# Node stage of a two-layer graph network: the second normalisation moved from VectorE to ScalarE

## Chip, cores and metric

The kernel runs on one core of a Trainium2 chip. The metric is the device time of one execution in microseconds (us), as the median of several runs.

## What is computed

There are 12500 nodes with 128 features and 200000 edges sorted by destination. Two layers follow each other. The first sums weighted neighbour rows per source node, sends the sums and the node's own row through a linear map with bias and relu, normalises both, adds them to the input row and normalises the row again. The second gathers a linear image of those rows per edge, and so on. The part that matters here is the end of the first layer:

```
h    = relu(feat_neigh @ W_neigh.T + b_neigh)                 # per node, 128 features
base = x + first branch + offsets
y    = base + scale * (h - mean(h)) / sqrt(var(h) + 1e-9)     # first normalisation (of h)
x1   = (y - mean(y)) / sqrt(var(y) + 1e-5)                    # second normalisation (of y)
f    = x1 @ node_w * attr                                     # rows for the second layer
```

## The kernel before

The program has four parts in order of time: a short set-up, a first edge stage (until about 3072 us), the **node stage** (3072 to 3357 us), a second edge stage (3357 to 5345 us) and a final stage over the nodes (to the end). The parts are separated by barriers, so a microsecond that the node stage takes more or less goes straight to the end.

The node stage cuts the 12500 rows into 25 blocks of 512 rows: 128 partitions with CB = 4 rows of 128 features each. Every engine runs its own list of instructions in order, written as a function `body(b)` that is called for b = 0, 1, 2, ... by `sweep` (unrolled before body 8 and after body 23, a loop between). A body handles several blocks of different age, and semaphores order the engines. `done(engine, signal, m)` waits until block m has given the signal. For block m the work is:

- SyncE loads the first of four tables of sums into `t_in` (L768), GpSimd adds the other three with accumulating DMAs in its bodies m+1, m+3 and m+5 (L789).
- TensorE, body m: 4 transposes of `t_in` (L811). Body m+1: bias and linear map into `ps_mm` (L818, L821), after the transposes of block m+1. Body m+4: 4 transposes of x1 out of `pack` (L829). Body m+5: 8 multiplications with `node_w` (L836).
- ScalarE, body b, in this order: clear a piece of `table` (L853), copy `nT` of block b (L856), relu of block b-1 into `h` (L861), square root for the h of block b-2, square root for the y of block b-3 (both L846, function `root`), copy `x1T` of block b-4 (L868), two DMA issues for block b-6 (L872, L873), eight scaled copies of block b-5 into `pack` and `f_sb` (L879, L881).
- VectorE, body b, in this order: `statistics` of the h of block b-2 and of the y of block b-3 (L892, L897, L901), then `centre` for the h of block b-2, then `centre` for the y of block b-3. A `centre` waits for the square root, takes the reciprocal (L905), refines it by one Newton step of three small instructions (L93, L95, L97; `refine`), and writes (row - mean) * rs with 4 instructions (L909), for h in place and for y into `pack`.
- GpSimd, body m+8: once h of block m is centred, y = h * scale (L796), y = y + base (L800); then, in its next body, three more accumulating DMAs.

The wait of ScalarE for `m_x1` does not exist before the change: x1 is VectorE's, and TensorE (L829) and GpSimd wait for it. The final stage already has a normalisation of the other form: VectorE makes a bias `nb` = -mean * rs (L1258), and ScalarE writes 4 copies with that bias and scale (L1214).

Of the kernel before, what the change touches and what calls it, by code (L numbers as in the profile page):

```python
# [15 lines left out]
ALU = mybir.AluOpType  # L16
ACT = mybir.ActivationFunctionType
# [20 lines left out]
NP = P  # L38
CB = 4
# [29 lines left out]
def at(s, q, j, back, ring=UN):  # L69

    return s - back, q + (j - back) // ring, (j - back) % ring
# [7 lines left out]
def done(eng, signal, step, back=0):  # L79

    if not isinstance(step, int) or step >= back:
        eng.wait_ge(signal, step - back + 1)  # L82


def uses(eng, signal, rnd, each):

    if not isinstance(rnd, int) or rnd > 0:
        eng.wait_ge(signal, rnd * each)


def refine(dve, v, r0, t, r, steps, m):

    dve.scalar_tensor_tensor(out=t[:, 0, :], in0=r0, scalar=-0.5, in1=v, op0=ALU.mult, op1=ALU.mult).then_inc(steps, 1)  # L93
    dve.wait_ge(steps, m * 3 + 1)
    dve.tensor_tensor(t[:, 1, :], t[:, 0, :], r0, ALU.mult).then_inc(steps, 1)  # L95
    dve.wait_ge(steps, m * 3 + 2)
    dve.scalar_tensor_tensor(out=r, in0=t[:, 1, :], scalar=1.5, in1=r0, op0=ALU.add, op1=ALU.mult).then_inc(steps, 1)  # L97
    dve.wait_ge(steps, m * 3 + 3)


def graph_layers(nc, a, out):
    with ExitStack() as ctx:
# [3 lines left out]
        def sem(name):  # L106
            return ctx.enter_context(nc.semaphore(name))

        def bank(name, shape, scope):
            return scope.enter_context(nc.psum_tensor(name, shape, F32))  # L110
# [40 lines left out]
        with ExitStack() as s0:  # L151
            def tmp(name, shape, dt=F32):
                return s0.enter_context(nc.sbuf_tensor(name, shape, dt))
# [8 lines left out]
            rows = tmp("rows", [1, 4, D])  # L162
# [202 lines left out]
        def live(b):  # L365
            return not isinstance(b, int) or 0 <= b < NB
# [23 lines left out]
        with ExitStack() as s2:  # L390
# [31 lines left out]
            mv = tmp("mv_s", [NP, HC, 2])  # L422
# [4 lines left out]
            rs = tmp("rs_s", [NP, HC])  # L427
# [293 lines left out]
        with ExitStack() as s3:  # L721
# [7 lines left out]
            y = tmp("y_m", [NP, 2, CB, D])  # L729
            pack = tmp("pack", [NP, UN, CB, 2, D])  # L730
# [3 lines left out]
            mv = tmp("mv_m", [NP, 2, CB, 2])  # L734
# [2 lines left out]
            r0 = tmp("r0_m", [NP, 2, CB])  # L737
            nw = tmp("nw_m", [NP, 2, 2, CB])
            rs = tmp("rs_m", [NP, 2, CB])
            ps_m = [bank(f"ps_mm{i}", [NP, CB, D], s3) for i in range(2)]  # L740
            ps_n = bank("ps_mn", [P, CB, P], s3)
            ps_t = bank("ps_mt", [P, CB, P], s3)
# [2 lines left out]
            pk_st = [sem(f"m_pk_st{i}") for i in range(UN)]  # L745
# [9 lines left out]
            m_cen, m_hs, m_y, m_x1 = sem("m_cen"), sem("m_hs"), sem("m_y"), sem("m_x1")  # L755
# [6 lines left out]
            with nc.Block() as block:  # L762
# [77 lines left out]
                @block.scalar  # L840
                def _(act):
                    def root(m, which):
                        if live(m):
                            done(act, m_var[which], m)
                            done(act, m_rs[which], m, 1)
                            act.activation(sd[:, which, :], var[:, which, :], ACT.Sqrt).then_inc(m_sd[which], 1)  # L846

                    clear = table[:, :, :].rearrange("p g n -> p (g n)")
                    act.wait_ge(m_blank, 1)

                    def body(b, q, j):
                        if live(b):
                            act.copy(clear[:, bass.ds(b * (2 * NT // NB), 2 * NT // NB)], blank[:, :]).then_inc(cleared, 1)  # L853
                            done(act, m_sum, b)
                            done(act, m_mm, b, 2)
                            act.copy(nT[:, j % 2, :, :], ps_n[:, :, 0:NP]).then_inc(m_nT, 1)  # L856
                        m, r, i = at(b, q, j, 1)
                        if live(m):
                            done(act, m_mm, m)
                            done(act, m_hs, m, 2)  # L860
                            act.activation(h[:, i % 2, :, :], ps_m[i % 2][:, :, :], ACT.Relu).then_inc(m_relu, 1)  # L861
                        root(b - 2, 0)
                        root(b - 3, 1)
                        m, r, i = at(b, q, j, 4)
                        if live(m):
                            done(act, m_tr, m)
                            done(act, m_f, m, 2)
                            act.copy(x1T[:, i % 2, :, :], ps_t[:, :, 0:NP]).then_inc(m_x1T, 1)  # L868
                        m, r, i = at(b, q, j, 6)
                        if live(m):  # L870
                            done(act, m_pk, m)
                            act.dma_start(rows_of(xs_d, m), pack[:, i, :, :, :].rearrange("p c g d -> p (c g d)")).then_inc(pk_st[i], 16)  # L872
                            act.dma_start(rows_of(f_d, m), flat(f_sb[:, i, :, :])).then_inc(pk_st[i], 16)  # L873
                        m, r, i = at(b, q, j, 5)
                        if live(m):
                            done(act, m_f, m)
                            uses(act, pk_st[i], r, 32)
                            for c in range(CB):
                                act.activation(pack[:, i, c, 1, :], ps_f[i % 2][:, c, 0:D], ACT.Copy,  # L879
                                               scale=attr_s[:, bass.ds(m * CB + c, 1)])  # L880
                                last = act.activation(f_sb[:, i, c, :], ps_f[i % 2][:, c, D:2 * D], ACT.Copy,  # L881
                                                      scale=attr_s[:, bass.ds(m * CB + c, 1)])
                            last.then_inc(m_pk, 1)
                    sweep(act, body, 0, NB + 6, 8, 24)
                    for i in range(UN):
                        act.wait_ge(pk_st[i], 32 * len(range(i, NB, UN)))

                @block.vector
                def _(dve):
                    def statistics(m, rows, which, eps):  # L890
                        for c in range(CB):
                            last = dve.bn_stats(st6[:, which, c, :], rows[:, c, :])  # L892
                        last.then_inc(m_st[which], 1)
                        dve.wait_ge(m_st[which], m * 2 + 1)
                        settle(dve, passed)
                        for c in range(CB):
                            last = dve.bn_aggr(mv[:, which, c, :], st6[:, which, c, :])  # L897
                        last.then_inc(m_st[which], 1)
                        dve.wait_ge(m_st[which], m * 2 + 2)
                        done(dve, m_sd[which], m, 1)  # L900
                        dve.tensor_scalar(var[:, which, :], mv[:, which, :, 1], eps, None, ALU.add).then_inc(m_var[which], 1)  # L901

                    def centre(m, rows, to, which):
                        done(dve, m_sd[which], m)
                        dve.reciprocal(r0[:, which, :], sd[:, which, :]).then_inc(m_rs[which], 1)  # L905
                        done(dve, m_rs[which], m)
                        refine(dve, var[:, which, :], r0[:, which, :], nw[:, which, :, :], rs[:, which, :], m_nw[which], m)
                        for c in range(CB):
                            last = dve.tensor_scalar(to[:, c, :], rows[:, c, :], mv[:, which, c, 0:1], rs[:, which, c:c + 1],  # L909
                                                     ALU.subtract, ALU.mult)  # L910
                        return last

                    def body(b, q, j):
                        m1, r1, i1 = at(b, q, j, 2)
                        m2, r2, i2 = at(b, q, j, 3)
                        if live(m1):
                            done(dve, m_relu, m1)
                            statistics(m1, h[:, i1 % 2, :, :], 0, 1e-9)
                        if live(m2):
                            done(dve, m_y, m2)  # L920
                            statistics(m2, y[:, i2 % 2, :, :], 1, 1e-5)
                        if live(m1):
                            k = i1 % 2
                            centre(m1, h[:, k, :, :], h[:, k, :, :], 0).then_inc(m_cen, 1)
                        if live(m2):
                            uses(dve, pk_st[i2], r2, 32)
                            centre(m2, y[:, i2 % 2, :, :], pack[:, i2, :, 0, :], 1).then_inc(m_x1, 1)
                    sweep(dve, body, 0, NB + 3, 8, 24)


# [361 lines left out]
```

## Time and profile before

| | us |
|---|---|
| median of 3 runs (5498.08 to 5500.08) | 5498.28 |
| the profiled execution | 5497.89 |
| its span in the trace | 5496.1 |
| node stage in it, 3072 to 3357 | 285 |

The span is that of the trace; the profiled execution's own time is 1.8 us longer. In the rows below, a row of the timeline gives the start, the duration (for several merged instructions from the first start to the last end), the engine, the line, what is written and read, the count, and in brackets the idle time of the engine before it and what ended it. PE is TensorE, PEld its weight loads, DVE VectorE, ACT ScalarE, ACTq the queue of ScalarE where it issues DMAs, POOL GpSimd. Successive instructions of an engine overlap by a part of their duration, so what one costs its engine in a row of equals is the distance between starts.

### The profile page before, as it was taken

To read this page: it belongs to the slowest core of one execution; us is meant where nothing else is said; L and a number is where in the kernel's file an instruction comes from. 1 tells how busy PE (TensorE), PEld (TensorE's weight loads), DVE (VectorE), ACT (ScalarE), POOL (GpSimd) and SP (SyncE) were. 2 spreads that over 40 slices of the span, in tenths; PEclk is the share of its full clock that TensorE was granted. 3 is DMA by queue.
4 is the path that set the end of the run, shared out by engine and by line. 5 is a ranking of instruction groups with operands and counts; after the bars stand their busy time and mean duration, and the time that the engine had idled before them with its cause. 6 is when DMAs were issued, how large, how long until landed. Compare 5 with 4: busy or idle time off the path is not lost. (4 is left out here: it accounts for less than half of the span.)

```text
span 5496.1 us, 83091 instructions
## 1 busy us (share of the span) xinstructions
PE 3528.2 (64%) x18413; PEld 2923.1 (53%) x18413; DVE 2741.1 (50%) x11175; ACT 2615.7 (48%) x9201; POOL 4067.5 (74%) x3277
## 2 busy tenths in 40 slices
PE   1555555555555555555555377888888888888872
PEld 0443343344334334334434255888888888888871
DVE  2655555555565555565555384333333333333338
ACT  0322222222222222222222255888888888888863
POOL 0888888888888888888888654777777777777750
PEclk9766666666666666676677577777777777777765
DMA  8666666666666666666665683333333333333323
GB/s 225 120 117 111 111 116 114 112 112 112 111 117 115 111 111 115 116 111 112 112 113 99 130 204 105 81 81 79 81 81 79 81 81 81 79 81 81 79 74 127
DMA packets 748229, 588.07 MB, mean 107 GB/s; under 512 B 336911, under 2 KB 616360, under 8 KB 745111
## 3 DMA queue, kind: packets, MB, share of 16 engines
q0 software_dynamic: 286576, 224.93, 29.6%
q1 hardware_dynamic: 446066, 310.47, 20.9%
q10 hardware_dynamic: 15542, 52.19, 2.4%
q8 instruction: 13, 0.21, 0.0%
q14 instruction: 32, 0.26, 0.0%
HBM read 374.65 MB, written 212.60 MB: 107 GB/s over the span
## 5 line engine op out<-in xcount | busy, mean ns | idle before, releaser
L705 POOL DMA_INDIRECT sums_scratch<-vals,to_i x1568 | 2447.4, 1561 | 616.5 <-issue 506.4
L992 POOL DMA_INDIRECT fg<-f_scratch,src_e x1568 | 1486.4, 948 | 501.6 <-issue 477.3
L1045 ACT ACTIVATE hot<-raw,e_s 128x40 f32<-128x40 f32 x6272 | 1392.3, 313 | 346.2 <-DVE raw L1068 317.5
L619 PE MATMUL ps_n<-same,hot 128*40 128x128 f32 x3136 | 694.3, 414 | 1326.8 <-issue 1324.9
L619 PEld LDWEIGHTS ps_n<-same,hot 128*40 128x40 f32 x3136 | 556.0, 184 | 1436.2 <-issue 1371.8
L662 ACT COPY near<-ps_n 40x512 f32<-40x512 f32 x196 | 113.3, 578 | 1636.3 <-PE ps_n L619 1636.3
L1021 PE MATMUL ps_eu<-hot,prod 128*128 128x120 f32 x3136 | 889.3, 378 | 0.0
L1019 PEld LDWEIGHTS ps_eu<-hot,prod 128*128 128x128 f32 x3136 | 622.3, 244 | 305.4 <-DVE prod L1075 253.9
L1074 DVE TENSOR_TENSOR prod<-ps_ew,fg 128x256 f32<-128x256 f32 x392 | 164.6, 420 | 1239.3 <-DMA fg<-f_scratch,src_e 1239.3
L1019 PE MATMUL ps_eu<-hot,prod 128*128 128x40 f32 x3136 | 618.9, 288 | 248.0 <-DVE prod L1075 247.0
L1021 PEld LDWEIGHTS ps_eu<-hot,prod 128*128 128x128 f32 x3136 | 619.6, 245 | 0.0
L586 DVE TENSOR_TENSOR to_i<-away,srcf 128x8 int32<-128x8 f32 x196 | 33.0, 169 | 1119.4 <-POOLq L76 1119.3
L573 DVE SCALAR_TENSOR_TENSOR junk<-srow_s,srcf,lower 128x128 f32<-128x128 int32 x1568 | 582.1, 437 | 0.0
L1008 PE MATMUL ps_ew<-fc_w,hid_e 128*128 128x256 f32 x1568 | 495.1, 472 | 13.3 <-DMA hid_e<-hid_scratch 13.3
L632 PEld LDWEIGHTS ps_v<-xw_s,near 40*128 40x128 f32 x3136 | 368.7, 190 | 205.4 <-issue 127.4
L632 PE MATMUL ps_v<-xw_s,near 40*128 40x128 f32 x3136 | 406.2, 280 | 0.9 <-ACT vals L673 0.9
L1008 PEld LDWEIGHTS ps_ew<-fc_w,hid_e 128*128 128x128 f32 x1568 | 365.3, 245 | 71.4 <-DMA hid_e<-hid_scratch 13.7
L561 DVE TENSOR_SCALAR same<-srow_s,srcf 128x128 f32<-128x128 int32 x1568 | 399.6, 340 | 4.5
L1075 DVE TENSOR_TENSOR prod<-ps_ew,fg 128x768 f32<-128x768 f32 x392 | 371.6, 948 | 0.0
L566 DVE TENSOR_SCALAR hot<-iota_f,rel,ew_s 128x40 f32<-128x40 f32 x1568 | 353.0, 340 | 0.0
L624 PE MATMUL ps_eh<-eT,fc_w 128*128 128x512 f32 x392 | 306.5, 873 | 0.0
L1030 PE MATMUL ps_ec<-sums,lin_w 128*128 128x80 f32 x1568 | 273.3, 335 | 0.0
(193 smaller groups left out, 3833.8 us busy)
## 6 DMA issues: line engine op xcount, KB each, us to landing
srow_s<-in_src SPq DMA_DIRECT2D x196, 512.0 KB, 3.5
e_s<-in_edge_attr SPq DMA_DIRECT2D x196, 256.0 KB, 3.7
hid_scratch<-hid SPq DMA_DIRECT2D x196, 256.0 KB, 3.6
hid_e<-hid_scratch SPq DMA_DIRECT2D x196, 256.0 KB
sums_scratch<-zeros ACTq DMA_DIRECT2D x24, 1056.0 KB, 26.8
sums_scratch<-vals,to_i POOLq DMA_INDIRECT x1568
fg<-f_scratch,src_e POOLq DMA_INDIRECT x1568
t_in<-sums_scratch POOLq DMA_DIRECT2D x72, 256.0 KB, 6.7
```

The costliest lines, as they stand in the source:

```text
L561: last = dve.tensor_scalar(same[:, k, t, :], rows[:, t // TH, t % TH, :], srcf[:, t:t + 1], None, ALU.is_equal)
L566: last = dve.tensor_scalar(hot[:, k, t, :], iota_f[:, 0:W], rel[:, t // TH, t % TH:t % TH + 1], ew_s[:, j, t:t + 1], ALU.is_equal, ALU.mult)
L573: last = dve.scalar_tensor_tensor(out=junk[:, t, :], in0=rows[:, t // TH, t % TH, :], scalar=srcf[:, t:t + 1], in1=lower[:, :], op0=ALU.is ...
L619: last = pe.matmul(ps_n[t // TH][:, t % TH, :], hot[:, k, t, :], same[:, k, t, :], start=True, stop=True)
L632: last = pe.matmul(ps_v[t // TH][:, t % TH, :], near[:, k, t, :], xw_s[:, i, t // TH, :], start=True, stop=True)
L705: pool.indirect_dma_start(out=sums_d[i], out_offset=bass.IndirectOffsetOnAxis(ap=to_i[:, j, t:t + 1], axis=0), in_=vals[:, j, t, :], in_of ...
L992: pool.indirect_dma_start(out=fg[:, j, t, :], out_offset=None, in_=f_d, in_offset=bass.IndirectOffsetOnAxis(ap=src_s[:, j, t:t + 1], axis= ...
L1008: last = pe.matmul(ps_w[k][:, 2 * t:2 * t + 2, :, :], hid[:, j, t, :], fc2_w[:, :], start=True, stop=True)
L1019: pe.matmul(ps_u[k][:, hf, 0, :], prod[:, k, t, 0, :], hot[:, k, t, 0, :], start=(t == 0), stop=False, skip_group_check=True)
L1021: last = pe.matmul(ps_u[k][:, hf, 1:4, :], prod[:, k, t, 1, :], hot[:, k, t, 1:4, :], start=False, stop=(t == TS - 1), skip_group_check=True)
L1045: last = act.activation(hot[:, k, t, c, :], raw[:, k, t, :], ACT.Copy, scale=e4_s[:, j, t, c:c + 1])
L1075: last = dve.tensor_tensor(prod[:, k, :, g, MUL:D].rearrange("p t (d u) -> p t d u", d=3), ps_w[k][:, :, 2 + g, None, :].to_broadcast([P, ...
```

## The change

VectorE no longer writes x1. It does the reciprocal and the refinement for y, then makes nb = -mean * rs, a 128x4 instruction, and signals `m_nb`. ScalarE waits for `m_nb` of block b-3 in its body b, behind the two square roots and ahead of the x1T copy, and writes the four 128x128 pieces of x1 as Identity with bias nb and scale rs. The wait for the store of the `pack` slot moves along with the writes. VectorE waits, ahead of the reciprocal for y, that ScalarE has written x1 of the block before, since `rs` and `nb` have one buffer. The additional `k = i1 % 2` changes nothing.

```diff
+            nb = tmp("nb_m", [NP, CB])
+            m_nb = sem("m_nb")
...
                         root(b - 2, 0)
                         root(b - 3, 1)
+                        m, r, i = at(b, q, j, 3)
+                        if live(m):
+                            done(act, m_nb, m)
+                            uses(act, pk_st[i], r, 32)
+                            for c in range(CB):
+                                last = act.activation(pack[:, i, c, 0, :], y[:, i % 2, c, :], ACT.Identity,
+                                                      bias=nb[:, c:c + 1], scale=rs[:, 1, c:c + 1])
+                            last.then_inc(m_x1, 1)
                         m, r, i = at(b, q, j, 4)
                         if live(m):
                             done(act, m_tr, m)
...
-                    def centre(m, rows, to, which):
+                    def inverse(m, which):
                         done(dve, m_sd[which], m)
                         dve.reciprocal(r0[:, which, :], sd[:, which, :]).then_inc(m_rs[which], 1)
                         done(dve, m_rs[which], m)
                         refine(dve, var[:, which, :], r0[:, which, :], nw[:, which, :, :], rs[:, which, :], m_nw[which], m)
+
+                    def centre(m, rows, to, which):
+                        inverse(m, which)
                         for c in range(CB):
...
                         if live(m2):
-                            uses(dve, pk_st[i2], r2, 32)
-                            centre(m2, y[:, i2 % 2, :, :], pack[:, i2, :, 0, :], 1).then_inc(m_x1, 1)
+                            done(dve, m_x1, m2, 1)
+                            inverse(m2, 1)
+                            dve.scalar_tensor_tensor(out=nb[:, :], in0=mv[:, 1, :, 0], scalar=-1.0, in1=rs[:, 1, :],
+                                                     op0=ALU.mult, op1=ALU.mult).then_inc(m_nb, 1)
```

## Rows read from the trace of the kernel before

**Rows 1.** Busy time by stretch: the node stage, and its late part.

```profile
core 0: us, PE busy (x) PEld busy (x) DVE busy (x) ACT busy (x) POOL busy (x), PEclk, DMA share, GB/s
3072.00:3357.00 285.00, 184.10 (x650) 128.17 (x650) 200.72 (x850) 125.50 (x350) 129.31 (x126) 0.69 0.73 182
3265.00:3317.00 52.00, 41.76 (x161) 30.05 (x160) 47.92 (x199) 29.94 (x86) 23.06 (x21) 0.76 0.55 150
```

**Rows 2.** Groups by line in the node stage: the transposes of the sums.

```profile
L811 PE MATMUL ps_mn<-ident,t_in 128*128 128x128 f32 x100 | 22.0, 360 | 128.0 <-DMA t_in<-sums_scratch 128.0
```

**Rows 3.** Timeline, VectorE, from one body's first reciprocal (body 14) to the next.

```profile
3223.90 0.18 DVE L905 RECIPROCAL r_m<-sd_m 128x4 f32<-128x4 f32 x1 [1.46 <-ACT sd_m L846]
...
3225.94 1.25 DVE L93 SCALAR_TENSOR_TENSOR nw_m<-r_m,var_m 128x4 f32<-128x4 f32 x1
...
3227.41 1.12 DVE L97 SCALAR_TENSOR_TENSOR rs_m<-nw_m,r_m 128x4 f32<-128x4 f32 x1
3228.57 1.11 DVE L909 TENSOR_SCALAR pack<-y_m,mv_m,rs_m 128x128 f32<-128x128 f32 x4
3229.60 0.86 DVE L892 BATCH_NORM_STATS2 st_m<-h_m 128x6 f32<-128x128 f32 x4
...
3232.62 0.17 DVE L905 RECIPROCAL r_m<-sd_m 128x4 f32<-128x4 f32 x1
```

**Rows 4.** Timeline, ScalarE: a pair from body 13, then bodies 14 and 15.

```profile
3213.86 0.57 ACT L868 COPY x1T<-ps_mt 128x512 f32<-128x512 f32 x1
...
3215.15 0.37 ACT L879 ACTIVATE pack<-ps_mf,attr_s 128x128 f32<-128x128 f32 x1 [0.72 <-issue]
...
3223.67 0.29 ACT L846 ACTIVATE sd_m<-var_m 128x4 f32<-128x4 f32 x2
3224.03 0.58 ACT L868 COPY x1T<-ps_mt 128x512 f32<-128x512 f32 x1
...
3227.54 0.37 ACT L879 ACTIVATE pack<-ps_mf,attr_s 128x128 f32<-128x128 f32 x1 [2.93 <-PE ps_mf L836]
...
3229.55 1.10 ACT L853 COPY table<-blank 128x1024 f32 x1
3230.49 0.65 ACT L856 COPY nT<-ps_mn 128x512 f32<-128x512 f32 x1
3230.97 0.67 ACT L861 ACTIVATE h_m<-ps_mm 128x512 f32<-128x512 f32 x1
3231.45 0.27 ACT L846 ACTIVATE sd_m<-var_m 128x4 f32<-128x4 f32 x1
```

**Rows 5.** Timeline, GpSimd and TensorE: from a centred h to the next sums.

```profile
3206.90 1.26 POOL L796 TENSOR_TENSOR y_m<-h_m,vecs 128x512 f32<-128x512 f32 x1 [5.28 <-DVE h_m L909]
...
3209.46 2.63 POOL L789 DMA_DIRECT2D t_in<-sums_scratch  x3
...
3218.02 1.11 PE L811 MATMUL ps_mn<-ident,t_in 128*128 128x128 f32 x4 [4.89 <-DMA t_in<-sums_scratch]
```

**Rows 6.** Timeline of the final stage: its bias on VectorE, its copies on ScalarE.

```profile
5409.60 0.16 DVE L1258 SCALAR_TENSOR_TENSOR nb_f<-mv_f,rs_f 128x4 f32<-128x4 f32 x1
...
5409.88 0.88 ACT L1214 ACTIVATE o_sb<-y_f,nb_f,rs_f 128x128 f32<-128x128 f32 x2 [3.20 <-DVE nb_f L1258]
5410.59 0.34 ACTq L1224 DMA_DIRECT2D out<-o_sb  x1
5410.66 0.86 ACT L1214 ACTIVATE o_sb<-y_f,nb_f,rs_f 128x128 f32<-128x128 f32 x2
5411.44 0.19 ACT L1220 ACTIVATE sd_f<-var_f 128x4 f32<-128x4 f32 x1
```

**Rows 7.** Timeline: first reciprocals of bodies 4 and 27, and the stage's last DMA issue.

```profile
3128.98 0.18 DVE L905 RECIPROCAL r_m<-sd_m 128x4 f32<-128x4 f32 x1 [4.45 <-ACT sd_m L846]
...
3342.61 0.18 DVE L905 RECIPROCAL r_m<-sd_m 128x4 f32<-128x4 f32 x1 [0.34 <-ACT sd_m L846]
...
3354.20 0.46 ACTq L873 DMA_DIRECT2D f_scratch<-f_sb  x1
```

More of the change, by code:

```diff
@@ L915, in body @@
                         m2, r2, i2 = at(b, q, j, 3)
+                        k = i1 % 2
                         if live(m1):
```

## The prediction

> **What bounds the kernel now.** I read the busy time by stretch first: the edit lies in the node stage alone, 285 us of the 5496.1 us span, in which VectorE is busy 201 us, ScalarE 125 us, and no engine is full [rows 1]. A stage in which nothing is full is bound by a ring of waits, so I went on to the timeline of one body on each engine, which I follow by the moment at which VectorE starts the body's first reciprocal (for h). In the middle of the stage it comes after 8.7 us and after 10.3 us by turns, 19.0 us for two bodies. Two things set it:
>
> - VectorE's own list. From the reciprocal at 3223.90 to the one at 3232.62 it never stops: 8.72 us [rows 3]. Two instructions of 128x4 take 1.25 and 1.12 us in it, as long as GpSimd's two multiplications and additions of y run beside them, where the same line takes 0.16 us elsewhere. The y half, from the first reciprocal to the first write of x1, is over 4.67 us after the body's start (3223.90 to 3228.57); the four writes themselves cost 1.03 us (3228.57 to 3229.60).
> - A ring through the sums. h is centred, GpSimd makes y (3206.90), issues the DMAs of the block four later (3209.46), TensorE gets them at 3218.02 [rows 5], then the linear map, relu and the square root of the block before lead to the reciprocal at 3223.90 [rows 3]. That is 17.0 us, and the 2.0 us from a reciprocal to GpSimd's start (3223.90 to 3225.94, where L93 begins to be held) make it 19.0 us for two bodies. The transposes waited 128 us for these DMAs in the stage, its start included [rows 2].
>
> ScalarE is on neither for long: in body 14 its copies started after 2.93 us of idling [rows 4].
>
> **The change, part by part.**
>
> 1. VectorE loses the four writes, 1.03 us a body [rows 3], and gains nb, 0.16 us with some 0.04 us of gap, as in the final stage [rows 6]. Its list shrinks from 8.72 to about 7.9 us. The nb instruction stands behind L97, which GpSimd's second operation has just released, so I give it 0.16 us; were it held as L93 is, it would be 1.25 us, which I keep for the range.
> 2. VectorE's new wait for x1 of the block before costs nothing: ScalarE wrote that in its body before, ahead of the square root that this body has already waited for.
> 3. ScalarE gains four Identity instructions. The final stage shows the same shape and operands: starts at 5409.88 and 5410.66 for two pairs, and the next instruction at 5411.44, so 1.56 us for four [rows 6]. The lower bound is the pitch of its copies with a scale alone, eight in 2.01 us (3227.54 to 3229.55), 1.0 us for four [rows 4]. I take 1.55, since function, source and operands are the same.
> 4. ScalarE gains a wait, and this decides. The wait for nb of block b-3 is met only at the **end** of VectorE's body b. Behind it in ScalarE's list stand all that the next body needs: x1T, two DMA issues, eight copies, the clear, nT, relu, and then the square root for which VectorE's body b+1 waits ahead of its first reciprocal. So the two lists, which ran side by side, now run one after the other: VectorE from the square root to nb, ScalarE from nb to the next square root.
>
> The sum for one turn of this new ring:
>
> - reciprocal to nb's start: 4.67 [rows 3]
> - nb's start to the first Identity: 0.28 (5409.60 to 5409.88) [rows 6]
> - four Identity: 1.55
> - x1T to the first copy: 0.48 to 1.29. Before it was 1.29 (3213.86 to 3215.15) with 0.72 idle for issue, since the queue put two DMA issues between [rows 4]. In the final stage a DMA issue goes out at 5410.59 while two Identity and a square root ahead of it are still to start [rows 6], so the queue runs ahead of its engine; here it has the 1.55 us of the Identities for that. I take 0.48, what a 128x512 copy costs in a row (3230.49 to 3230.97), and keep 1.29 for the range.
> - eight copies: 2.01; clear to nT: 0.94; nT to relu: 0.48; relu to square root: 0.48 (3229.55, 3230.49, 3230.97, 3231.45) [rows 4]
> - square root to reciprocal: 0.23 (3223.67 to 3223.90) [rows 4, 3]
>
> Together 11.1 us a body. VectorE's statistics of the next body (3.0 us, 3229.60 to 3232.62) lie beside ScalarE's 6.2 us and cost nothing. The ring through the sums needs 19.0 us for two bodies against 22.2 now, so it and TensorE's work fall into slack of 3 us.
>
> **The whole stage.** Body 4 starts, as before, at 3128.98 [rows 7], since it waits for the first DMAs of the ring. In body 4 ScalarE has no copies yet: 4.67 + 0.28 + 1.55 + 0.48 + 0.94 + 0.48 + 0.48 + 0.23 = 9.1, so body 5 starts at 3138.1, and with copies body 6 at 3149.2. Eighteen full turns of 11.1 lead to body 24 at 3349.0. Body 25 has no clear and no nT (9.7), bodies 26 and 27 no relu either (9.2 each): body 27 at 3377.1, against 3342.61 before [rows 7]. From there to the last DMA issue it was 11.6 us (3354.20); the wait chain at the end is nearly the same, with the four Identity in place of the four writes: plus 0.5. So the stage ends about **35 us** later, and the barrier behind it passes that on whole. Against the profiled execution's 5497.89 us that gives 5532.9; the median of the runs is 0.39 higher, and I put 5533.
>
> A page of the Trainium skill speaks the other way. Perfetto Trace Analysis, Optimizing Scalar/DVE Operations, says that where VectorE is saturated, offloading some of its work to ScalarE may make sense. By it this change should pay; the price that it would have here is the second rival's.
>
> **The rivals.**
>
> - *The ring with unhidden issues.* As forecast, but ScalarE's queue doesn't run ahead through the Identities: 0.8 us more in each of 21 turns, plus 17 us: 5550. For it: the 0.72 us of issue [rows 4]. Against it: the DMA issue between the Identities [rows 6]. Chance 0.13.
> - *The offload pays.* VectorE is at 47.9 of 52 us in the late part of the stage, ScalarE at 29.9 [rows 1]. There VectorE's list is the only bound, over the nine bodies from 3265 us on; if ScalarE took x1 without delaying the square root, each of these would be 0.83 us shorter, about 7 us in all, and at most 0.83 in each of 24, 20 us: 5491, at best 5478. The ring through the sums has no x1 in it and would not shorten. It decides from the point where the x1 copies end early enough that the next square root is ready when VectorE has its statistics, 3.0 us after nb; the list above needs 6.2 after the first Identity starts. For it only the low share of ScalarE, which is an average. Chance 0.03.
> - *No difference.* ScalarE's new wait falls into its idle time (2.93 us ahead of the copies in every second body [rows 4]) and the old ring stays the bound: 5498. Against it: that slack is used up by the Identities and the wait (nb at about 3228.7, when the copies had already begun at 3227.54), and the other body has none. Chance 0.04.
>
> The forecast has the remaining 0.80.
>
> **Range and chances.** The low end takes Identity at the copies' pitch (0.55 less in 21 turns, 11.5 us: plus 23) and some overlap that I don't see, 5512. The high end takes unhidden issues (5550) and a part of a held nb, 5556. This leaves out little more than the two rivals without a ring. A measurement of this kernel can tell about 0.2%, 11 us, from no change. The ring in either form is slower by more than that: 0.93. Within 0.2%: 0.04. Faster by over 0.2%: 0.03.
>
> **What the profile after would show.** If right: in the timeline of a middle body the first Identity starts 0.3 us behind nb, and ScalarE then runs without a gap to the square root; VectorE is idle some 3 us ahead of every first reciprocal, released by the square root, and the turn is 11.1 us in every body without the alternation; TensorE's wait for the DMAs shrinks and its wait for ScalarE grows. The stage takes about 320 us. If the DMA issues are not hidden there is idle time for issue between x1T and the first copy, and 11.9 us a turn. I am wrong if a first reciprocal follows the statistics without a gap, if the stage is no longer than 296 us, or if stages other than the node stage change by more than a microsecond or two.

## The result and the profile after

| | before | changed |
|---|---|---|
| median, us | 5498.28 (5 runs, 5496.1 to 5500.08) | 5527.75 (5 runs, 5526.98 to 5530.41) |
| span of the profiled execution, us | 5496.1 | 5525.2 |

The changed kernel is slower by 29.5 us: the ratio is 1.0057, with a 95% interval from 1.0044 to 1.0069. That is more than the 0.2% that a measurement of this kernel can tell.

First the busy time by stretch of the changed kernel; the first row is its node stage, the second its middle, the third its second edge stage (columns: length of the stretch, then busy time and count of instructions of each engine, clock, DMA share, GB/s):

```profile
core 0: us, PE busy (x) PEld busy (x) DVE busy (x) ACT busy (x) POOL busy (x), PEclk, DMA share, GB/s
3072.00:3392.00 320.00, 199.89 (x650) 137.66 (x650) 179.16 (x775) 158.24 (x450) 129.28 (x126) 0.64 0.64 160
3128.00:3265.00 137.00, 100.74 (x324) 69.57 (x323) 90.25 (x383) 74.08 (x211) 62.87 (x62) 0.66 0.72 175
3387.00:5375.00 1988.00, 1730.24 (x9800) 1614.80 (x9800) 684.49 (x1572) 1626.12 (x7262) 1479.79 (x1568) 0.76 0.32 81
```

VectorE lost 22 us of busy time (costed for 25 blocks: 21) and ScalarE gained 33 (costed: 39) [rows 1]. No engine is full: ScalarE is busy for 158 of 320 us, VectorE for 179. But ScalarE's gain is close to what the stage grew by, so busy time alone can't tell the added work from a wait. TensorE's granted clock was 0.64 in the stage where it was 0.69, and its busy time grew by 16 us, to 200. The waits say where the time is. This is the list of who waited for whom in the changed kernel's node stage (total us, times, longest):

```profile
POOL y_m L798 <- DVE h_m L922: 159.8, 25, 12.6
PE ps_mn L813 <- DMA t_in<-sums_scratch: 127.4, 21, 70.3
ACT pack L871 <- DVE nb_m L942: 116.6, 25, 4.9
PEld ps_mn L813 <- DMA t_in<-sums_scratch: 90.9, 7, 70.6
DVE r_m L915 <- ACT sd_m L848: 75.8, 25, 5.4
```

And the last of these in the kernel before:

```profile
DVE r_m L905 <- ACT sd_m L846: 21.4, 10, 5.2
```

ScalarE waits 25 times for nb, 4.7 us each time on average, and VectorE 25 times for ScalarE's square root, 3 us each, where it waited 10 times before. Waits of each engine for the other in every body are what two lists give that run one after the other; the timeline shows whether they do. One turn of that on VectorE, from the timeline, with a first reciprocal at either end:

```profile
3217.11 0.18 DVE L915 RECIPROCAL r_m<-sd_m 128x4 f32<-128x4 f32 x1 [2.83 <-ACT sd_m L848]
...
3219.15 1.24 DVE L93 SCALAR_TENSOR_TENSOR nw_m<-r_m,var_m 128x4 f32<-128x4 f32 x1
...
3220.62 1.12 DVE L97 SCALAR_TENSOR_TENSOR rs_m<-nw_m,r_m 128x4 f32<-128x4 f32 x1
...
3221.77 0.16 DVE L942 SCALAR_TENSOR_TENSOR nb_m<-mv_m,rs_m 128x4 f32<-128x4 f32 x1
3221.85 0.86 DVE L902 BATCH_NORM_STATS2 st_m<-h_m 128x6 f32<-128x128 f32 x4
...
3228.28 0.18 DVE L915 RECIPROCAL r_m<-sd_m 128x4 f32<-128x4 f32 x1 [3.31 <-ACT sd_m L848]
```

And the same turn on ScalarE:

```profile
3222.05 0.49 ACT L871 ACTIVATE pack<-y_m,nb_m,rs_m 128x128 f32<-128x128 f32 x1 [4.88 <-DVE nb_m L942]
3222.41 0.34 ACTq L882 DMA_DIRECT2D xs_scratch<-pack  x1
3222.45 0.86 ACT L871 ACTIVATE pack<-y_m,nb_m,rs_m 128x128 f32<-128x128 f32 x2
3222.92 0.34 ACTq L883 DMA_DIRECT2D f_scratch<-f_sb  x1
3223.22 0.48 ACT L871 ACTIVATE pack<-y_m,nb_m,rs_m 128x128 f32<-128x128 f32 x1
3223.61 0.56 ACT L878 COPY x1T<-ps_mt 128x512 f32<-128x512 f32 x1
3224.07 0.36 ACT L889 ACTIVATE pack<-ps_mf,attr_s 128x128 f32<-128x128 f32 x1
...
3226.08 1.09 ACT L855 COPY table<-blank 128x1024 f32 x1
3227.01 0.64 ACT L858 COPY nT<-ps_mn 128x512 f32<-128x512 f32 x1
3227.49 0.66 ACT L863 ACTIVATE h_m<-ps_mm 128x512 f32<-128x512 f32 x1
3227.98 0.36 ACT L848 ACTIVATE sd_m<-var_m 128x4 f32<-128x4 f32 x2
```

Where [rows 3] show the writes of x1 behind L97, there is now the small nb, and where ScalarE had its copies before it was idle until nb came; from the first Identity on it has no gap up to the square root. The turn is 3228.28 - 3217.11 = 11.17 us, and both DMA issues go out between the Identities. Since ScalarE has no gap there, it waits for nothing of TensorE's, and TensorE's lower clock did not make this turn.

Where the whole time went, from starts in the two profiles (the node stage from its first clear to its last DMA issue, L873 before; the gather from its first issue on GpSimd to its last):

| us | before | changed | difference |
|---|---|---|---|
| start to the first clear | 3072.74 | 3073.75 | +1.0 |
| node stage | 281.5 | 317.2 | +35.8 |
| last DMA issue to the first gather | 9.5 | 9.4 | -0.1 |
| gather of the second edge stage | 1963.0 | 1956.4 | -6.6 |
| last gather to the end | 169.4 | 168.5 | -0.9 |

The sum is +29.2. So the node stage alone gives more than the kernel lost, and the second edge stage, which the change does not touch, gave 6.6 us back.

### The profile page after: what moved, and what is told of

Same layout as the page of the kernel before. It is cut to its first block and busy times, and to the rows that moved or that the text cites. A ratio compares the mean times of both kernels' runs of the same rounds, so it can differ in the third digit from the quotient of the medians.

```text
span 5525.2 us, 83132 instructions
## 1 busy us (share of the span) xinstructions
PE 3520.1 (64%) x18413; PEld 2923.2 (53%) x18413; DVE 2718.1 (49%) x11100; ACT 2648.4 (48%) x9301; POOL 4063.3 (74%) x3277
## 5 line engine op out<-in xcount | busy, mean ns | idle before, releaser
L624 PE MATMUL ps_eh<-eT,fc_w 128*128 128x512 f32 x392 | 285.1, 815 | 0.0
```

## The experiments

The theory is the new ring of waits; its main rival is that the added work on ScalarE costs the time by itself. The first four kernels take the two apart.

**e1: the same work, the wait at the end of ScalarE's body.**

```diff
-                        m, r, i = at(b, q, j, 3)
-                        if live(m):
-                            done(act, m_nb, m)
-                            uses(act, pk_st[i], r, 32)
-                            for c in range(CB):
-                                last = act.activation(pack[:, i, c, 0, :], y[:, i % 2, c, :], ACT.Identity,
-                                                      bias=nb[:, c:c + 1], scale=rs[:, 1, c:c + 1])
-                            last.then_inc(m_x1, 1)
...
                             last.then_inc(m_pk, 1)
+                        m, r, i = at(b, q, j, 3)
+                        if live(m):
+                            done(act, m_nb, m)
+                            uses(act, pk_st[i], r, 32)
+                            for c in range(CB):
+                                last = act.activation(pack[:, i, c, 0, :], y[:, i % 2, c, :], ACT.Identity,
+                                                      bias=nb[:, c:c + 1], scale=rs[:, 1, c:c + 1])
+                            last.then_inc(m_x1, 1)
```

> The changed kernel with one thing moved: ScalarE waits for nb and writes the four pieces of x1 at the end of its body, behind the eight copies, not ahead of the x1T copy. The work is the same to the instruction. Theory (the new ring of waits costs the time): x1T, two DMA issues and eight copies, 2.5 us, leave the ring, which is then 4.67 + 0.28 + 1.55 + 0.94 + 0.48 + 0.48 + 0.23 = 8.6 us a body; VectorE's list is 7.9, so the old ring through the sums, 19.0 us for two bodies, sets the pace again: last DMA issue of the node stage within 8 us of before (3354), total 5490 to 5502. Rival (ScalarE's added work costs the time): nothing changes, 5528.

Measured: 5495.13 us, ratio to before 1.0001 (0.9991 to 1.001). The node stage is 286.3 us, 4.8 more than before, so 31.0 of the 35.8 us are gone with the instructions all there; the total is no longer at all, since the second edge stage is 6.6 us shorter than before here too. From its timeline, nb and what follows:

```profile
3295.70 0.41 ACT L883 ACTIVATE f_sb<-ps_mf,attr_s 128x128 f32<-128x128 f32 x1
3296.61 0.16 DVE L942 SCALAR_TENSOR_TENSOR nb_m<-mv_m,rs_m 128x4 f32<-128x4 f32 x1
...
3296.81 1.65 ACT L891 ACTIVATE pack<-y_m,nb_m,rs_m 128x128 f32<-128x128 f32 x4 [0.70 <-DVE nb_m L942]
...
3298.36 1.03 ACT L855 COPY table<-blank 128x1024 f32 x1
```

The eight copies are over when nb comes; ScalarE waits 0.70 us where it waited 4.88.

**e2: the wait without the work.** VectorE writes x1 as before.

```diff
+                        m, r, i = at(b, q, j, 3)
+                        if live(m):
+                            done(act, m_nb, m)
                         m, r, i = at(b, q, j, 4)
                         if live(m):
                             done(act, m_tr, m)
...
                         refine(dve, var[:, which, :], r0[:, which, :], nw[:, which, :, :], rs[:, which, :], m_nw[which], m)
+                        if which == 1:
+                            dve.scalar_tensor_tensor(out=nb[:, :], in0=mv[:, 1, :, 0], scalar=-1.0, in1=rs[:, 1, :],
+                                                     op0=ALU.mult, op1=ALU.mult).then_inc(m_nb, 1)
```

> The kernel before with the wait alone: VectorE makes nb (nothing reads it), signals it and then still writes x1 itself; ScalarE waits for nb at the place of the change and gets no new work. Theory: the ring closes without the Identities: 4.67 + 0.28 + 1.29 (x1T to the first copy, DMA issues no longer hidden) + 2.01 + 0.94 + 0.48 + 0.48 + 0.23 = 10.4 us a body against 11.1, so about 21 x 0.7 = 15 us less than the changed kernel in the node stage: 5510 to 5518, still slower than before by 12 to 20. Rival (the added work of ScalarE): as before, 5498.

Measured: 5512.04 us, ratio 1.003 (1.0019 to 1.0042); node stage 303.6 us, 22 more than before. The wait without the work costs it. On ScalarE, in the timeline of one body:

```profile
3283.08 0.58 ACT L873 COPY x1T<-ps_mt 128x512 f32<-128x512 f32 x1 [4.80 <-DVE nb_m L914]
3283.22 0.34 ACTq L877 DMA_DIRECT2D xs_scratch<-pack  x1
3283.73 0.34 ACTq L878 DMA_DIRECT2D f_scratch<-f_sb  x1
3284.26 0.37 ACT L884 ACTIVATE pack<-ps_mf,attr_s 128x128 f32<-128x128 f32 x1 [0.60 <-issue]
```

Without the Identities the two DMA issues are in the open again: 1.18 us from x1T to the first copy (3283.08 to 3284.26), against 0.46 in the changed kernel (3223.61 to 3224.07). A turn there is 10.6 us on average from body 6 to body 23, most of them 10.3 to 10.7 (forecast 10.4).

**e3: the work without the wait.** The output is unchanged; the four added instructions write a tile that nothing reads.

```diff
+                        m, r, i = at(b, q, j, 3)
+                        if live(m):
+                            for c in range(CB):
+                                last = act.activation(spill[:, i % 2, c, :], blank[:, D * c:D * (c + 1)], ACT.Identity,
+                                                      bias=spare[:, 0:1], scale=attr_s[:, c:c + 1])
+                            last.then_inc(m_sp, 1)
                         m, r, i = at(b, q, j, 4)
```

> The kernel before with the work alone: ScalarE does four Identity instructions of 128x128 with bias and scale operands at the place of the change, out of a constant tile into one that nothing reads, without any wait; VectorE is as before. Theory: most of the 1.55 us a body falls into ScalarE's idle time; the node stage is longer by 0 to 8 us, 5498 to 5506. Rival (the added work): 21 x 1.55 = 33 us longer, 5530.

Measured: 5495.45 us, ratio 1.0 (0.999 to 1.0009); node stage 283.6 us, 2.1 more than before. The groups by line of its node stage show the same amount of work as L871 does in the changed kernel, 479 ns each (482 there):

```profile
L869 ACT ACTIVATE spill<-blank,spare,attr_s 128x128 f32<-128x128 f32 x100 | 40.8, 479 | 0.0
...
L887 ACT ACTIVATE pack<-ps_mf,attr_s 128x128 f32<-128x128 f32 x100 | 37.6, 376 | 6.3 <-PE ps_mf L838 4.8 <-ACT f_sb L889 1.0 <-issue 0.5
```

The same copies in the kernel before:

```profile
L879 ACT ACTIVATE pack<-ps_mf,attr_s 128x128 f32<-128x128 f32 x100 | 38.0, 380 | 31.9 <-PE ps_mf L836 26.6 <-issue 4.3 <-ACT f_sb L881 1.0
```

ScalarE's idle time ahead of its copies, for TensorE's result, is 4.8 us here and was 26.6; the added work went mostly into time in which ScalarE stood still. The rival has fallen.

**e4: the change, with VectorE's y half ahead of its h half**, so that nb is made early.

```diff
+                        if live(m2):
+                            done(dve, m_x1, m2, 1)
+                            inverse(m2, 1)
+                            dve.scalar_tensor_tensor(out=nb[:, :], in0=mv[:, 1, :, 0], scalar=-1.0, in1=rs[:, 1, :],
+                                                     op0=ALU.mult, op1=ALU.mult).then_inc(m_nb, 1)
                         if live(m1):
                             k = i1 % 2
                             centre(m1, h[:, k, :, :], h[:, k, :, :], 0).then_inc(m_cen, 1)
-                        if live(m2):
-                            done(dve, m_x1, m2, 1)
-                            inverse(m2, 1)
-                            dve.scalar_tensor_tensor(out=nb[:, :], in0=mv[:, 1, :, 0], scalar=-1.0, in1=rs[:, 1, :],
-                                                     op0=ALU.mult, op1=ALU.mult).then_inc(m_nb, 1)
```

> The changed kernel with VectorE's two halves swapped: reciprocal, refinement and nb for y come ahead of the centring of h. Theory: nb comes 1 us after the square root and not 4.67, so the new ring is about 7.4 us and no longer the bound; L93 and L97 of y no longer run beside GpSimd, so they take 0.16 us each and VectorE's list falls to some 6 us. The ring through the sums gets the 1 us of the y half: about 20 us for two bodies, 10.0 a body against 9.3 on average before: 5500 to 5515. Rival (ScalarE's work): 5528.

Measured: 5502.0 us, ratio 1.0011 (1.0001 to 1.002); node stage 292.8 us. As forecast: the new ring is gone, and the ring through the sums, longer by the y half, is the bound: until body 17 first reciprocals come after 7.5 us and after 12.6 to 14.0 us by turns, about 20.4 us for two bodies where it was 19.0. Its VectorE timeline at a first reciprocal:

```profile
3211.27 0.18 DVE L915 RECIPROCAL r_m<-sd_m 128x4 f32<-128x4 f32 x1 [6.11 <-ACT sd_m L848]
3211.48 0.16 DVE L93 SCALAR_TENSOR_TENSOR nw_m<-r_m,var_m 128x4 f32<-128x4 f32 x1
...
3211.88 0.16 DVE L97 SCALAR_TENSOR_TENSOR rs_m<-nw_m,r_m 128x4 f32<-128x4 f32 x1
3212.07 0.16 DVE L939 SCALAR_TENSOR_TENSOR nb_m<-mv_m,rs_m 128x4 f32<-128x4 f32 x1
```

nb starts 0.80 us after the reciprocal and not 4.66. The h half that no longer stands between is 1.8 us of that, and the other 2 come from L93 and L97, which no longer run beside GpSimd's two operations: 0.16 us each in place of 1.24 and 1.12.

The next four kernels shorten the rings, to see whether each part of the sum stands, and whether the offload can pay.

**e5: the kernel before, with the square root for h at the start of ScalarE's body.**

```diff
                     def body(b, q, j):
+                        root(b - 2, 0)
                         if live(b):
...
-                        root(b - 2, 0)
                         root(b - 3, 1)
```

> The kernel before with ScalarE's square root for h moved from behind the relu to the start of its body; no offload. Theory: it takes the relu of the next block out of the way of the centring, so the ring through the sums spans three bodies, (18.9 + 1.7) / 3 = 6.9 us a body, and VectorE's list, 8.72 us, is the only bound: every body 8.7 us without alternation, last DMA issue some 13 us earlier, 5483. Rival (the list of VectorE was the bound all along): no change, 5496.

Measured: 5476.65 us, ratio 0.9965 (0.9952 to 0.9978). The body is 8.72 us without alternation (first reciprocals at 3206.60, 3215.32 and 3224.04), as said; the node stage is 261.6 us, 19.8 less than before where I expected 13: the bodies from 4 to 27 give 12.1, and body 4 starts 7.7 us sooner after the stage's first clear, which I had not counted. So before the change the bound in every second body, up to body 18, was the ring through the sums, and what closed it over two bodies was one small square root queued behind a relu.

**e6: the changed kernel with the same move.**

```diff
                     def body(b, q, j):
+                        root(b - 2, 0)
                         if live(b):
...
-                        root(b - 2, 0)
                         root(b - 3, 1)
```

> The changed kernel with the same move of the square root for h. Theory: clear, nT and relu (1.9 us) leave the new ring, which is then 4.67 + 0.28 + 1.55 + 0.48 + 2.01 + 0.23 = 9.2 us a body in place of 11.1: last DMA issue 40 us earlier than in the changed kernel, about 5488. If something else than this ring made the 11.1 us, it stays above 5515.

Measured: 5485.87 us, ratio 0.998 (0.997 to 0.999); node stage 274.8 us, 42 less than the changed kernel. The turn is the 9.2 us of the sum:

```profile
3274.13 0.18 DVE L915 RECIPROCAL r_m<-sd_m 128x4 f32<-128x4 f32 x1 [1.05 <-ACT sd_m L848]
...
3278.80 0.16 DVE L942 SCALAR_TENSOR_TENSOR nb_m<-mv_m,rs_m 128x4 f32<-128x4 f32 x1
...
3279.08 0.49 ACT L871 ACTIVATE pack<-y_m,nb_m,rs_m 128x128 f32<-128x128 f32 x1 [2.97 <-DVE nb_m L942]
...
3283.11 0.25 ACT L848 ACTIVATE sd_m<-var_m 128x4 f32<-128x4 f32 x1
...
3283.38 0.18 DVE L915 RECIPROCAL r_m<-sd_m 128x4 f32<-128x4 f32 x1 [1.39 <-ACT sd_m L848]
```

It is 9 us slower than e5, its twin without the offload, and its stage is 13.1 us longer: with the wait in that place the offload costs, in either order of the roots.

**e7: e6, and the x1 pieces at the end of ScalarE's body as in e1.** Against the changed kernel:

```diff
                     def body(b, q, j):
+                        root(b - 2, 0)
...
-                        root(b - 2, 0)
                         root(b - 3, 1)
-                        m, r, i = at(b, q, j, 3)
-                        if live(m):
-                            done(act, m_nb, m)
-                            uses(act, pk_st[i], r, 32)
-                            for c in range(CB):
-                                last = act.activation(pack[:, i, c, 0, :], y[:, i % 2, c, :], ACT.Identity,
-                                                      bias=nb[:, c:c + 1], scale=rs[:, 1, c:c + 1])
-                            last.then_inc(m_x1, 1)
...
                             last.then_inc(m_pk, 1)
+                        m, r, i = at(b, q, j, 3)
+                        if live(m):
+                            done(act, m_nb, m)
+                            uses(act, pk_st[i], r, 32)
+                            for c in range(CB):
+                                last = act.activation(pack[:, i, c, 0, :], y[:, i % 2, c, :], ACT.Identity,
+                                                      bias=nb[:, c:c + 1], scale=rs[:, 1, c:c + 1])
+                            last.then_inc(m_x1, 1)
```

> The changed kernel with the square root for h at the start of ScalarE's body and the pieces of x1 at its end. Theory: both rings are slack (the new one 4.67 + 0.28 + 1.55 + 0.23 = 6.7 us, the one through the sums 6.9), and VectorE's shortened list of 7.9 us is the bound: here the offload pays, last DMA issue some 32 us earlier than before, about 5465. Rival (ScalarE's added work costs time by itself): no better than e5.

Measured: 5473.21 us, ratio 0.9956 (0.9941 to 0.9971); node stage 265.5 us. This is a miss: not 5465, and in the profiles the stage is 3.8 us longer than e5's; the total lies 3.4 us below e5's all the same, with a second edge stage that is 5.2 us shorter. The timeline of VectorE and, of the same moments, of ScalarE shows what I left out:

```profile
3209.72 0.17 DVE L915 RECIPROCAL r_m<-sd_m 128x4 f32<-128x4 f32 x1
...
3217.51 0.17 DVE L915 RECIPROCAL r_m<-sd_m 128x4 f32<-128x4 f32 x1
...
3218.31 1.12 DVE L922 TENSOR_SCALAR h_m<-h_m,mv_m,rs_m 128x128 f32<-128x128 f32 x4
3223.33 0.18 DVE L915 RECIPROCAL r_m<-sd_m 128x4 f32<-128x4 f32 x1 [3.91 <-ACT sd_m L848]
```

```profile
3222.54 0.60 ACT L864 ACTIVATE h_m<-ps_mm 128x512 f32<-128x512 f32 x1 [3.42 <-PE ps_mm L823]
3223.03 0.20 ACT L848 ACTIVATE sd_m<-var_m 128x4 f32<-128x4 f32 x1
```

A body is 7.8 us where nothing disturbs it (3209.72 to 3217.51), the shortened list as forecast, and 9.0 on average from body 6 to body 23. But the square root for **y** still stood behind the relu, and VectorE's y half, which is ahead of the next h, waited 3.91 us for it.

**e8: both square roots at the start of ScalarE's body, and VectorE's y half first, as in e4.** ScalarE's part of the edit, against the changed kernel; VectorE's is e4's:

```diff
                     def body(b, q, j):
+                        root(b - 2, 0)
+                        root(b - 3, 1)
                         if live(b):
...
-                        root(b - 2, 0)
-                        root(b - 3, 1)
```

> The changed kernel with VectorE's y half first (as in e4) and both square roots at the start of ScalarE's body. Theory: VectorE's list about 6 us, ScalarE's 6.3, the new ring under 7, the ring through the sums (20.6 + 1.5 + 1.0) / 3 = 7.7 us a body as the bound: about 5460. If TensorE at 1.2 GHz becomes the bound (its list is then 9.9 us a body) it is no faster than before.

Measured: 5460.47 us, ratio 0.9935 (0.9917 to 0.9952), the fastest of all and 36 us below before. The node stage is 250.9 us, 30.5 less than before; the agreement with the forecast of 5460 is partly luck, since the second edge stage, which the forecast left as it was, gave 6.5 us. Late in the stage a body takes 7.5 us (first reciprocals at 3279.54 and 3287.01), and 8.4 on average from body 6 to body 23, where 7.7 was forecast. Here the offload is in place and the stage is 10.7 us shorter than e5's, though e8 changes the order too, so this difference is not the offload's alone; the same orders without the offload were not run, and what it is worth by itself stays open.

**r1 to r4: both kernels twice more.** Nothing is edited in them. They were to tell whether the 6.6 us of the second edge stage belong to the program.

> The kernel before, once more, for its second edge stage. In the first profile 24 of its 1568 gather issues on GpSimd took 1.5 us from start to start and not 1.25 (6.5 us in all); in the changed kernel none did. If the program decides (its phase between VectorE and GpSimd is the same in every execution), this run has 18 to 24 of them and the stage is 5 to 6.5 us longer than in r2; if it is chance, the number is another one in each run.

> The changed kernel, once more. Node stage of 317 us within 2 us, as in the first profile. If the program decides, none of its gather issues in the loop is stretched and the stretch from first to last issue is 1956.4 us; if it is chance, some are.

> The kernel before, a third profile, with the same two readings as in r1: 18 to 24 stretched issues if the program decides, any number if it is chance.

> The changed kernel, a third profile, with the same two readings as in r2: none stretched if the program decides, any number if it is chance.

Measured: 6545.03, 6572.96, 6520.74 and 6582.96 us. All four are some 1000 us longer than every run above, and so was the kernel before that ran beside them (6555.8 us); nearly all of it lies in the second edge stage, whose gather took 2956 to 2992 us. In each of the four GpSimd waits there 97 to 100 times, 928 to 1029 us in all, for the loads of the edge indices (`src_e`), for which it waits only once in the kernel before, at the start of the stage; why those loads were late stays open. All four ran on another chip than e1 to e8. They can't answer the question they were made for. Their node stages are undisturbed and repeat the first profiles: 282.4 and 283.3 us before, 318.2 and 317.7 us changed, so the stage is 35.1 us longer, against 35.8 in the first pair.

## Why the prediction was right

The direction, the place and the mechanism are as forecast, and 5527.75 us lies in the range, 5.3 us below the number.

- **The ring.** Forecast 11.1 us a turn, measured 11.17 and, over 17 turns from body 6 (3150.47) to body 23 (3340.00), 11.15 on average. Term by term: reciprocal to nb 4.66 (forecast 4.67), nb to the first Identity 0.28 (0.28), four Identities 1.56 (1.55), x1T to the first copy 0.46 (0.48), eight copies 2.01 (2.01), then 0.93, 0.48 and 0.49 (0.94, 0.48, 0.48), and 0.30 to the reciprocal (0.23). The last is the only one that moved by more than 0.02: the square root itself took 0.26 us here and 0.20 in the row of the forecast; why is not shown.
- **The choice of 0.48 over 1.29** for x1T to the first copy was right, and it decided between the forecast and the first rival (5550). e2 shows the other value, 1.18, as soon as the Identities are gone.
- **The Identity at 1.55 and not 1.0** was right: source and operands as in the final stage gave the same duration.
- **nb at 0.16 us** was right: it starts as GpSimd's second operation ends, and was held in no body.
- **The stage.** Forecast about 35 us longer, measured 35.8, and 35.1 in the repeated pair. Body 27 starts at 3379.16 (forecast 3377.1), and from there to the last DMA issue it is 11.8 us (forecast 12.1). Of the 2 us, 1.4 are in the start of body 4 (3130.37 for 3128.98) and the rest in the turns.
- **What failed** is the step that carried the stage to the end whole, and the sentence that other stages would not change by more than a microsecond or two. The second edge stage became 6.6 us shorter; without that the kernel would have come to about 5534. The 5.3 us between forecast and result come from there; the node stage alone was forecast to about 1 us. One smaller sign failed too: TensorE's wait for the DMAs of the sums did not shrink (127.4 us, and 128.0 before), though its wait for ScalarE grew as said, to 33 us for x1T and, in its weight loads, 37 us for x1.
- **The rivals.** "The offload pays" fell: e6 is slower than e5. The rule of the Trainium skill (Perfetto Trace Analysis, Optimizing Scalar/DVE Operations) that offloading to ScalarE may make sense where VectorE is saturated did not hold for this change, whose VectorE list became shorter (22 us less busy) and whose stage became longer. Over the whole stage VectorE was busy for only 70% of the time before, but also late in it, at 47.9 of 52 us [rows 1], where its list was the only bound, the turn went from 8.7 to 11.1 us. e7's undisturbed body of 7.8 us against e5's 8.72 shows what it is worth where the wait does not close a ring. "No difference" would have needed the wait in ScalarE's slack; e3 shows that the work does fit there (2.1 us), e2 that the wait does not (22 us).

## What to carry to other kernels

Before work is moved to an engine with idle time, ask when its operand is ready and what is queued behind the wait. A wait for the last result of another engine's round, placed ahead of work that the other engine needs for its next round, makes the two run in series: a turn is then the sum of the two stretches, however little work was moved. Put such a wait at the end of the list, or make its operand first; and look for a small instruction that stands behind an unrelated late one, as the square root behind the relu here, whose move took 19.8 us from the stage. The offload made the stage longer in each of the four pairs of kernels that differ in nothing else: by 35.8 us, and by 4.8 with its wait at the end of the list (e1); with the square root moved, by 13.1 (e6 against e5) and 3.8 (e7 against e5).

## What the runs showed of the hardware beyond that

The 6.6 us come from GpSimd's gather issues. In the kernel before, 24 of 1568 issues took about 1.5 us from start to start where the others take 1.25; all 24 are the fifth issue of a round of 32. In the timeline of the kernel before, one of them beside VectorE:

```profile
3528.64 0.49 DVE L1068 TENSOR_TENSOR raw<-iota_f,rel 128x320 f32<-128x320 f32 x1
...
3528.72 1.23 POOL L992 DMA_INDIRECT fg<-f_scratch,src_e  x1 [0.30 <-issue]
```

And the same place of the round in the changed kernel:

```profile
3565.36 0.95 POOL L1008 DMA_INDIRECT fg<-f_scratch,src_e  x1 [0.30 <-issue]
3565.44 0.49 DVE L1084 TENSOR_TENSOR raw<-iota_f,rel 128x320 f32<-128x320 f32 x1
```

Where this instruction of VectorE's starts 0.05 to 0.31 us ahead of the issue, the issue takes 1.00 to 1.26 us, longest where they are closest; where it starts 0.04 us ahead or less, after the issue, or 0.40 us ahead or more, 0.94 to 0.96. In the ten profiles from before to e8 there are 490 fifth issues: all 67 with such a lead are stretched, and none of the other 423. Two more readings say that one waits for the other. Every stretched issue ends 1.31 us after VectorE's start (1.305 to 1.318), whatever its own start. And in the 61 pairs in which VectorE leads by 0.04 us or less it is VectorE's instruction that is longer, 0.52 to 0.57 us in place of 0.49.

A page of the Trainium skill, SBUF — State Buffer, SBUF: two separate sides, says that VectorE and GpSimd share a pair of ports as an exclusive lock, which whoever starts first holds for its whole instruction; for a VectorE instruction with two inputs in SBUF, as this one, it says so only against a GpSimd operation that reads SBUF. The trace agrees in that one of the two waits, and a shift of 0.1 us decides over 0.3 us. It differs in how long GpSimd holds: a VectorE instruction that starts 0.08 us behind an issue of 0.95 us takes its usual 0.49 us, as in the row above. That what the issue reads in SBUF is its list of indices, `src_e`, is my reading; no run shows it apart. The same lock would explain L93 and L97: before, 48 of their 100 executions are long, all of them beside a running operation of GpSimd's, and each ends 0.02 us behind it; in e4 none runs beside one, and none is long.

Which kernels have it goes with the program in these ten profiles: 24 stretched issues before, 18 in e3 and 18 in e5, none at that place beyond the stage's second round in the changed kernel, e1, e2, e4, e6, e7 and e8, whose gathers all took 1956.4 to 1956.6 us. The first three are the ones in which VectorE makes no nb in the node stage. Why an instruction there should shift the phase of the two engines in the next stage by 0.1 us was not found, and the repeats meant to tell program from chance were no use for it. So part of the distance to before, 5 to 7 us in every comparison above with a kernel that makes nb, is not the node stage's: e1's 4.8 us longer stage and its unchanged total are such a case.
